# A four-layer network on one core: PSUM buffers from a fixed table instead of fitted due times, and three seams woven anew

## The reference, cut to what matters

```python
x = x + _layernorm(_L0_attn_ref(_layernorm(x, axis=-1), ...), axis=-1)   # 16 heads of 8, low-rank weights, then a gelu MLP
x = x + _layernorm(_L0_ffn_ref(_layernorm(x, axis=-1), ...), axis=-1)    # dense FFN + 4 heads x top-8 of 512 experts
x = x + _layernorm(_L1_attn_ref(_layernorm(x, axis=-1), ...), axis=-1)   # 16 heads of 8
x = x + _layernorm(_L1_ffn_ref(_layernorm(x, axis=-1), ...), axis=-1)    # 6 x (local attention, window 32, rotary; gated gelu FFN)
```

## Time and profile before

| | before |
|---|---|
| median of 3 runs | 4216.69 us (4215.99 to 4220.44) |
| the profiled execution | 4219.54 us, span 4218.2 us |
| PE busy | 3821.9 us (91%) |
| DVE, ACT, POOL busy | 3337.9, 3335.4, 2871.2 us |

### The profile page before, as it was taken

One profiled execution on the slowest core, in us unless ns is written; L12 is line 12 of the kernel. 1 busy time (PEld: TensorE's weight loads), 2 busy tenths in 40 slices (PEclk: granted clock), 3 DMA queues, 4 the chain that ended last, 5 costly groups with the idle time before them and its releaser, 6 DMA issues.

```text
span 4218.2 us, 149280 instructions
## 1 busy us (share of the span) xinstructions
PE 3821.9 (91%) x62848; PEld 3004.1 (71%) x62848; DVE 3337.9 (79%) x6090; ACT 3335.4 (79%) x5144; POOL 2871.2 (68%) x2624
## 2 busy tenths in 40 slices
PE   7887566657887999999999999999999999999998
PEld 5666445446664777777777777777777777777787
DVE  5665999884656988888888888888888888888884
ACT  4665788885555888888888888888888888888885
POOL 1222888883446887777777777777777777777773
PEclk9999787888998999999999999999999999999999
DMA  2000000000000111111111111111111111111111
GB/s 68 3 2 2 1 1 1 1 1 31 3 3 4 37 27 26 32 37 21 30 33 38 21 28 26 36 33 25 30 33 38 21 28 25 36 23 25 29 24 38
DMA packets 191912, 96.89 MB, mean 23 GB/s; under 512 B 167888, under 2 KB 180880, under 8 KB 191120
## 3 DMA queue, kind: packets, MB, share of 16 engines
q1 hardware_dynamic: 191248, 87.34, 9.2%
HBM read 23.89 MB, written 2.10 MB: 6 GB/s over the span
## 4 chain that ended last, share of the span: by engine, by line
PE 75%; ACT 7%; POOL 6%; issue 5%; DVE 5%; ACTq 0%; DVEq 0%; POOLq 0%
PE ps L1480 16%; PE ps L1468 9%; PE ps L1416 9%; PE ps L1417 8%; PE ps L1446 7%; PE ps L1425 4%; PE ps L1457 3%; PE ps L1534 3%; PE ps L1515 3%; PE ps L1523 3%; PE ps L397 2%; ACT arena L567 2%; PE ps L1436 2%; PE ps L446 1%; POOL arena L241 1%
## 5 line engine op out<-in xcount | busy, mean ns | idle before, releaser
L1781 POOL TENSOR_TENSOR arena<-arena 128x1024 f32<-128x1024 f32 x384 | 910.2, 2370 | 52.2 <-DVE arena L1676 46.6
L1800 POOL TENSOR_TENSOR arena<-arena 128x1024 f32<-128x1024 f32 x192 | 365.0, 1901 | 595.9 <-DVE arena L1704 595.9
L1787 POOL TENSOR_TENSOR arena<-arena 128x1024 f32<-128x1024 f32 x384 | 726.3, 1902 | 7.3 <-ACT arena L1572 7.0
L1480 PEld LDWEIGHTS ps<-arena 128*128 128x128 f32 x6144 | 713.6, 192 | 20.7 <-issue 3.2
L1480 PE MATMUL ps<-arena 128*128 128x128 f32 x6144 | 717.2, 275 | 0.0
L1675 DVE TENSOR_TENSOR arena<-ps,arena 128x1024 f32<-128x1024 f32 x384 | 468.7, 1221 | 201.9 <-ACT arena L1556 192.4
L1676 DVE TENSOR_TENSOR arena<-ps,arena 128x1024 f32<-128x1024 f32 x384 | 466.6, 1215 | 0.0
L1684 DVE TENSOR_REDUCE arena<-arena 128x32 f32<-128x2048 f32 x192 | 437.0, 2276 | 0.0
L239 POOL TENSOR_SCALAR arena<-arena 128x2 f32<-128x2 f32 x256 | 71.5, 279 | 527.8 <-DVE arena L233 516.7
L1416 PE MATMUL ps<-arena 128*128 128x512 f32 x768 | 415.0, 622 | 6.8 <-DVE arena L1676 2.7
L1582 ACT ACTIVATE arena<-ps 128x1024 f32<-128x1024 f32 x192 | 196.7, 1024 | 281.1 <-PE ps L1457 281.1
(11 more groups left out here) (251 smaller groups left out, 8744.2 us busy)
## 6 DMA issues: line engine op xcount, KB each, us to landing
arena<-arena SPq DMA_DIRECT2D x96, 256.0 KB
arena<-arena SPq DMA_DIRECT2D x480, 32.0 KB
arena<-in_dWqk SPq DMA_DIRECT2D x12, 512.0 KB, 6.0
arena<-arena SPq DMA_DIRECT2D x96, 64.0 KB
arena<-arena SPq DMA_DIRECT2D x96, 63.5 KB
arena<-in_dWvT SPq DMA_DIRECT2D x6, 512.0 KB, 4.2
arena<-in_dWo SPq DMA_DIRECT2D x6, 512.0 KB, 5.1
arena<-arena SPq DMA_DIRECT2D x192, 0.2 KB
```

The costliest lines, as they stand in the source:

```text
L1480: i = pe.matmul(p[:, 0:128], o[:, u, c, :], w[:, u, c, :], start=(u == c == 0), stop=(u == 1 and c == 7))
L1781: pool.tensor_tensor(a1[:, half], a1[:, half], T2[:, half], ALU.add).then_inc(*radd[g].up())
L1787: pool.tensor_tensor(a3, a3, bc(ss[:, 16 * g:16 * g + 16], 2, 64), ALU.mult).then_inc(*nrm[g].up())
```

## The change

There are three edits, all in the tables that decide buffers and order; no operation is added or removed, and the number of matmuls is the same.

```diff
 class Slots:
-    def __init__(self, n):
+    def __init__(self, n, plan=""):
+        self.plan = [int(x) for x in reversed(plan)]
         self.last, self.until, self.place, self.prev = [None] * n, [-1e9] * n, {}, {}
 
     def take(self, use, until, beside=None):
-        i = min((n for n in range(len(self.until)) if n != beside), key=lambda n: self.until[n])
+        if self.plan:
+            i = self.plan.pop()
+        else:
+            i = min((n for n in range(len(self.until)) if n != beside), key=lambda n: self.until[n])
         self.place[use], self.prev[use] = i, self.last[i]
@@
-    C.psum, lines = Slots(4), []
+    C.psum, lines = Slots(4, PLAN), []
@@
+PLAN = ("0123012301203012301203210312301230123023120132310213021320132130120313021032103120312310320131023012"
...
-TURNS = [[[1, 15, 9, 11, 4, 15, 29, 21], [1, 13, 2, 2, 1, 25, 1, 8, 3, 12, 18, 23], ...
+TURNS = [[[1, 15, 9, 25, 4, 1, 29, 21], [1, 6, 2, 9, 1, 33, 4, 12, 18, 23], ...
```

More of the change, by code:

```diff
@@ L67 @@
 LAST = 5952
-TIMES = {"a": [[-6000, -24], [0, 10], [1000, 16], [2000, 30], [3000, 46], [5000, 85], [8000, 146], [12000, 227], [14000, 268], [15000, 288], [16000, 309], [17000, 327], [18000, 347]], "b": [[-6000, 69], [0, 326], [500, 348], [1000, 360], [1500, 380], [2000, 398], [3000, 431], [4000, 465], [6000, 533], [10000, 668], [14000, 804], [15000, 838], [16000, 872], [17000, 901], [18500, 928]], "c": [[-6000, 857], [0, 904], [1000, 912], [2000, 929], [3000, 947], [5000, 985], [8000, 1042], [12000, 1117], [14000, 1155], [15000, 1174], [16000, 1192], [17000, 1212], [18000, 1232]], "d": [[-9000, 1206], [0, 1206], [1000, 1206], [2000, 1206], [3000, 1217], [4000, 1230], [5000, 1235], [6000, 1248], [7000, 1257], [8000, 1267], [9000, 1280], [10000, 1290], [11000, 1304], [12000, 1315], [14000, 1340], [18000, 1387], [23000, 1451]]}
@@ L73 @@
-TURNS = [[[1, 15, 9, 11, 4, 15, 29, 21], [1, 13, 2, 2, 1, 25, 1, 8, 3, 12, 18, 23], [2, 34, 7, 18, 2, 1, 1, 7, 1, 1, 11, 17, 3, 3, 12, 3, 3, 2], [7, 17, 9, 6, 16, 6, 21, 3], []], [[3, 4, 1, 3], [1, 71, 5, 3, 1, 8], [8, 20], [1, 13, 1, 12], []], [[3, 3, 6, 6, 11, 3, 1, 23, 14, 2, 2, 10], [12, 23, 11, 2, 1, 14], [2, 38, 11, 2, 2, 2, 2, 4, 11, 14, 4, 2, 15, 2], [2, 44, 4, 2, 8, 35, 13, 1, 2, 10, 4, 9], []]]
+TIMES = {"a": [[-6000, -32], [0, 15], [1000, 22], [2000, 37], [3000, 57], [5000, 100], [8000, 169], [12000, 260], [14000, 306], [15000, 329], [16000, 352], [17000, 374], [18000, 398]], "b": [[-6000, 20], [0, 373], [500, 402], [1000, 412], [1500, 433], [2000, 450], [3000, 483], [4000, 517], [6000, 584], [10000, 717], [14000, 851], [15000, 885], [16000, 919], [17000, 950], [18500, 981]], "c": [[-6000, 868], [0, 950], [1000, 963], [2000, 982], [3000, 1001], [5000, 1041], [8000, 1100], [12000, 1180], [14000, 1219], [15000, 1239], [16000, 1258], [17000, 1282], [18000, 1308]], "d": [[-9000, 1284], [0, 1284], [1000, 1284], [2000, 1284], [3000, 1290], [4000, 1305], [5000, 1309], [6000, 1323], [7000, 1332], [8000, 1342], [9000, 1355], [10000, 1365], [11000, 1379], [12000, 1391], [14000, 1416], [18000, 1467], [23000, 1533]]}
@@ new lines @@
+PLAN = ("0123012301203012301203210312301230123023120132310213021320132130120313021032103120312310320131023012"
+        "3013201321301203310230123013201321301203310230123013201321301203310230123013201321301203310230123013"
+        "2013213012033102301230132013213012033102301230132013213012033102301230132013213012033102301230132013"
+        "2130120331023012301320132130120331023012301320132130120312301320130132013201231032103210321301230123"
+        "0123012301230123012301230123012301230123012301230123012301230123012301230123012301230123012301230123"
+        "0123032103120132031023120321301201230132103201302312012031230213012310320120132031023120321301201230"
+        "1321032013023120120312302130123103201201320310231203213012012301321032013023120120312302130123103201"
+        "2013203102312032130120123013210320130231201203123021301231032012013203102312032130120123013210320130"
+        "2312012031230213012301032121012312211212103111321302102321021303200113123120030130112301301302130130"
+        "132301201201320120120301231231")
@@ L76 @@
+TURNS = [[[1, 15, 9, 25, 4, 1, 29, 21], [1, 6, 2, 9, 1, 33, 4, 12, 18, 23], [2, 53, 7, 7, 2, 1, 12, 17, 1, 3, 3, 3, 8, 2], [7, 17, 9, 6, 15, 6, 10, 3], []], [[3, 4, 1, 3], [1, 60, 5, 3, 1, 8], [8, 20], [1, 13, 1, 12], []], [[3, 2, 5, 9, 12, 4, 1, 19, 14, 2, 2, 10], [10, 10, 2, 8, 10, 5, 2, 16], [2, 51, 11, 4, 4, 4, 11, 14, 4, 2, 15, 2], [2, 44, 3, 2, 1, 13, 8, 22, 13, 1, 2, 10, 4, 9], []]]
 class Signal:
```

## The result

Slower: 4239.17 us (median of 5, 4235.39 to 4241.62) for 4216.69 (4215.78 to 4220.77); the ratio is 1.0046, 95% interval 1.0035 to 1.0057, so +19.4 us (14.8 to 24.0); the two medians are 22.5 apart. The profiled execution took 4236.63 us, 17.1 more than the one of before, and its span is 4235.3 us.

The account below looks back on a forecast made before the run. PE was taken to bound the kernel, 91% busy, with movable time in stages a, c and the seams. 9.1 + 13.2 - 1.5 + 0 - 7 + 1 = +14.8 us gave 4231.5 us, range 4212 to 4243 for 8 in 10.

Parts of the forecast that it names:

- z and s1, +9.1: Stage a: s1 starts 0.70 us later behind ACT's second instruction in 13 batches, z's delay adds nothing; 9.1 us slower.
- m2, +13.2: Stage a: m2 waits for the gelu, 1.37 us late, leaving c 1.1 late in 12 batches; 13.2 us slower.
- Seam a to b, -1.5: Seam a to b: m1.14 3.2 us earlier, first top-8 4.8 later, nearly cancelling; 1.5 us faster.
- Stage c, 0: Stage c: exchanged holders are pairs both waited for, or pieces read out before; no change.
- Seam c to d, -7: Seam c to d: c.14, m.15 and w.14 go ahead of q0.1, stage d moves earlier; 7 us faster.
- g0.15 about 6 us sooner: Seam c to d: sign of being right, the first exponent scores starting about 6 us sooner after s1.15.
- Stage d, +1: Stage d: of 21 changed takes most at the seam, two look late at 0.7 to 1.4 each; 1 us slower.
- an absorbed m2 wait: Rival, stage a: ACT is late at cT by itself, so m2's term vanishes; +1.6 us, 4218; chance 0.12.
- That the holders' order doesn't matter: Rival, stage a: neither late-holder term counts, only the seams remain; 4209; chance 0.08.
- The larger seam: Rival, seam c to d, PE between 1286 and 1331: -18.6 us for -7, 4207; chance 0.10.
- The clock's fall: Rival, stage a: TensorE's clock falls in the longer rounds, 11 us more, 4242; chance 0.08.
- a grant under 1.00 in the steady part: Sign of being wrong: PE's granted clock under 1.00 in the steady part of stage a.

Follow-up runs that it names:

- e3: Changed kernel with the old holders of m2, qkv, c, w and g3 in stage a, z and s1 as changed; 4229.25 us, ratio to before 1.0020.
- e10: Kernel before, with only s1 inheriting late in stage a (half a of g2, in 13 batches); 4235.60 us, ratio to before 1.0042.
- e11: Kernel before, with only z inheriting late in stage a (half b of g2, in 13 batches); 4224.36 us, ratio to before 1.0012.
- e2: Changed kernel with the old holders of z, s1 and s0 in stage a, m2 and qkv as changed; 4226.13 us, ratio to before 1.0011.
- e5: Kernel before with the change's order and holders at the seam from a to b; 4221.07 us, ratio to before 1.0007.
- e12: Kernel before with g3a and g3b exchanging holders in 14 batches of stage c; 4223.00 us in one run, before beside it 4215.25.
- e6: Kernel before with the change's order and holders at the seam from c to d; 4215.99 us, ratio to before 0.9991.
- e4: Changed kernel with the old holders in stage d's tiles from the seam on; 4237.24 us, ratio to before 1.0036.
- e1: Changed kernel with all of stage a's holders as before; 4217.09 us, ratio to before 0.9993.
- e7: Kernel before with the change's holders in stages b and c only; 4218.27 us, ratio to before 0.9999.
- e9: Changed kernel with stage a's and stage d's holders as before, both new seams and stage c's holders kept; 4217.59 us, ratio to before 0.9988.

## Why the prediction was right, and where its sizes were off

The forecast, slower by 14.8 us to 4231.5, came out on the right side by the right mechanism, in stage a. The time lies 7.7 us above it.

- *z and s1, +9.1.* Right: rounds of 23.10 with s1 alone late (e3, e10), 0.70 each as worked out from ACT's pair, 13 times. z's delay adds nothing behind a late s1 (e10 and e3 have the same round) and 0.33 in front of an early one (e11).
- *m2, +13.2.* Right in kind, 1.1 us too large: in e2 m2 was 1.42 late for 1.37, c 1.06 and ACT's read of it 1.03 for 1.1, so the round grew by 1.01 and twelve rounds by 12.1. That the round which ends the stage gives 1.3 back wasn't in the forecast.
- *Seam a to b, -1.5.* Wrong in sign, as far as e5 tells: +3.0. Both ends were worked out rightly (3.2 earlier on PE, 4.8 later for the first top-8; measured 3.3 and 5.0). The step that failed is "the two nearly cancel. I take -1.5, nearer to neither end": the earlier trace rows had DVE idle 9.63 us for that very top-8, and the lateness of what hangs on it is what was left at the end of stage b.
- *Stage c, 0.* Right in sum by luck: a gain of 1.2 and a loss of 1.4 us cancel, and I had seen neither. "PE waits for both halves before the first matmul of either" is true, and yet the order in which it does so cost 0.16 a round (e12).
- *Seam c to d, -7.* -4.4 (e6). "g0.15 about 6 us sooner" was 6.3; 1.0 of it went up to pp.15, where q1.1 waits 0.95 between the exponent groups, which the step named and didn't subtract, and 0.9 in stage d's start-up, for "all of d moves with it".
- *Stage d, +1.* +3.0 (e4 against the change). The step was "two look late, at 0.7 to 1.4 each"; four wait, and one of them, t0.5, stands 2.91 us where e4 stands 1.03, because it inherits from the piece directly in front of it. Its other half, "most are at the seam", is a miscount: 23 takes of stage d have another holder, 6 at the seam and 17 in the tiles up to the sixth, the ones that e4 puts back.

With these, 9.1 + 12.1 - 1.3 + 3.0 + 0 - 4.4 + 3.0 = +21.5 us, for 22.5 between the medians and 17.1 between the two profiles. That the sum comes so near the medians is in part luck, for the two profiles don't go by it: the change is 22.8 late at g2.14 of stage a, 21.5 at pp.15, 21.7 at the end of b (where the sum has 3.0 more), 21.9 at g2.14 of c, 15.3 at g0.15, 20.2 at d's seventh tile and 17.1 at the end, behind the same instructions in the same order.

The rivals: an absorbed m2 wait is refuted by e2, whose rounds are 1.01 longer with m2 alone late. That the holders' order doesn't matter is refuted by e1, e10 and e11: with the same four buffers and the same order of pieces in the round it is 22.40, 22.73, 23.10 or 24.12 us, according to whom a piece inherits from. The larger seam is refuted by e6. The clock's fall, of which the forecast had said that a grant under 1.00 in the steady part would be a sign of being wrong, happened in one round of the change's profile (25.62 us for 24.11, near 309 us) and one of e4's, 1.5 us and not the 11 of the rival; it was rounds of 23.1 that met it most.

The Trainium skill, page Perfetto Trace Analysis, section Identifying Performance Opportunities, says that a gap which repeats on the engine that should be busy can mean too little space for the next tile. Here the gap does repeat, 1.34 us in front of m2 and 1.06 in front of z, and it is a wait for a PSUM buffer; e1 takes both away with no buffer more (0.69 in front of s1 stays).

## What to carry to other kernels

A rotation of buffers is judged by the last instruction that reads a holder, in the order of the reading engine, against the time at which the heir's turn comes on its own engine: one instruction later in ACT's pair was worth 0.70 us in every round, the gelu's end instead of DVE's read 1.01. Late holders add up along an in-order queue when each lies behind the other's slack, and a piece should not inherit from the piece directly in front of it. At a seam, look for an engine that has been idle long for the next stage's first result (9.63 us here), and be slow to put anything ahead of what that result waits for; a seam, a stage and its start-up are best measured one by one, since +3.0, +3.0 and -4.4 us looked like nothing together. And the order of two buffers that are waited for at one matmul counts: here it was 0.15 us cheaper to have the one that comes free last in the last wait.

## What the runs showed of the hardware

*The clock falls in one execution and not in the next, in the same program.* e6 has the same instructions as the kernel before up to stage c, yet its last round of a, from g2.14 to g2.15, took 26.37 us for 24.61. The windows of before and then of e6:

```profile
378.00:384.00 6.00, 2.70 (x66) 2.05 (x70) 3.24 (x15) 4.23 (x8) 1.25 (x4) 1.00 0.00 0
384.00:390.00 6.00, 4.54 (x114) 3.50 (x118) 0.30 (x2) 3.50 (x6) 1.30 (x2) 1.00 0.01 3
```

```profile
378.00:384.00 6.00, 3.04 (x46) 2.21 (x46) 3.27 (x15) 3.46 (x8) 1.09 (x3) 0.82 0.00 0
384.00:390.00 6.00, 4.79 (x82) 3.29 (x82) 0.55 (x2) 3.53 (x6) 1.46 (x3) 0.61 0.01 3
```

In both PE stands idle for about half of the first six microseconds; in e6 the grant went to the lower level (1.2 GHz) for part of the time, and pp.15 came 2.4 us later. e1 and e5 show the same fall, e7, e9 and the kernel before don't. A difference of 2 us between two profiles is therefore nothing by itself, and it is why the terms above are taken between points of a profile that lie close together.

*Rounds of 23.1 us met the lower clock more often than longer ones.* In the stretch from 113 us to g2.14, rounds at a fall: four in e3 and two in e10 (both 23.10 when undisturbed), one each in the change and e4 (24.12), none in e2 (23.41), e11 (22.73) and before (22.40). Ahead of that stretch it is another picture: in the round that ends near 91 us before, e7, e9 and e12 took 23.3 to 23.5 us (granted 0.92 in the window 82 to 104, for before), while e1, e5, e6 and e11 took 22.3 to 22.5 (granted 1.00). One profile of each kernel isn't enough to call this a rule.

*The order of a matmul's waits costs time.* With the same four semaphores, the last one to come in the first of two wait instructions instead of the second made 0.15 us between its release and the matmul (e12, where the two take 51 ns each and start 0.11 us apart). The Trainium skill, page Perfetto Trace Analysis, section Identifying Dependency Chains, says that an instruction which waits for several engines may have further instructions with the other conditions put in front of it. The trace agrees: two such instructions stand in front of this one, and which of them has the late condition is worth the 0.25 us for 0.10.
